# A Macaron block of routed experts and a selective scan: one more pair of buffers for delta*x, whole-group products by B, and a rearranged start

## The chip, the cores and the metric

The kernel runs on one core of a Trainium2 chip, as one launch. The metric is device time in microseconds (us) of one execution; lower is better. The five engines are called by the profile's names: PE (TensorE; PEld is its weight load), DVE (VectorE), ACT (ScalarE), POOL (GpSimd) and SP (SyncE), which here issues DMAs and nothing else.

## What is computed

4096 tokens (2 sequences of 2048) of width 1024 in float32 go through a layer norm and a routed feed-forward, a layer norm and a selective scan, and a third layer norm with the same feed-forward again, each added to its input.

```python
x = x + 0.5 * ffn(layernorm(x), A, B, W, bias)
x = x + scan(layernorm(x), W_xproj, W_dt, b_dt, A_log, D_param)
x = x + 0.5 * ffn(layernorm(x), A, B, W, bias)

def ffn(x, A, B, W, bias):            # A: 64 experts x rank 16 x 1024, top 4 of 64
    vecs = einsum('arh,bsh->bsar', A, x)
    routes = one_hot(top_k(norm(vecs, axis=-1), 4)).sum(-2) / 4
    v = einsum('bsa,bsar->bsr', routes, vecs)
    return x @ W.T + bias + einsum('bsa,ajr,bsr->bsj', routes, B, v)

def scan(x, W_xproj, W_dt, b_dt, A_log, D):   # state 16, rank 128
    xz = x @ W_xproj.T                        # delta_r | B_mat | C_mat
    delta = softplus(delta_r @ W_dt.T + b_dt)
    h_t = exp(delta_t * -exp(A_log)) * h_(t-1) + delta_t * B_t * x_t
    return (sum over n of h_t * C_t) + x * D
```

## The kernel before

**Units.** The work of the two feed-forwards is cut into 64 units of 128 tokens, numbered 0 to 63: 32 of kind 1 (the first feed-forward, and then the projections of the scan) and 32 of kind 2 (the second, on what the scan gives). In a unit a, PE multiplies for the base (`base`, x by W), for the routed part (`routed`, u by B) and, for the next unit b, for the experts (`experts`, x by A). Each weight is held as two float16 parts, high and low, and each product is three: high by high, high by low, low by high. All engines have a hand-written order: `unit(l, a, b)` of each engine's block, with l the unit before.

**Scan groups.** The scan's rows are (channel, state) pairs: a tile t is 128 channels of 512 tokens (64 tiles), and has 4 groups, so there are 256 groups G = 4t + g. A group is four blocks of 128 rows x 512 tokens. Its way: `times_b` (POOL) multiplies delta*x by B into a ring `Hr` of four groups; `decay` (ACT) makes exp(delta*A) into PSUM, two blocks ahead at most; `scan` (DVE) runs the recurrence; `keep_last` (ACT) copies the last column of the four blocks to `hst` for the next chunk and lets `times_c` (POOL) multiply by C in place; `states` (PE) sums over the states into `py`; `sum_up` (DVE) adds x*D. The table that `plan` makes spreads the groups over the units 5 to 57, five a unit in most, four in nine of them (units 5, 10, 16, 22, 28, 34, 40, 46, 52); those of a unit are its slots 0 to 4. POOL does `times_b(G + 2)` ahead of `times_c(G)`.

**The tile's inputs.** delta of tile t is made one or two units ahead: `z` (PE, by a slice of `wdt`, all of W_dt held), `magnitudes` and `softplus` (ACT), `delta` (DVE, which multiplies by the normed x that `load_tile` fetched), `delta_copy`, and `delta_out` (ACT stores delta and delta*x to a scratch in memory, semaphore `s_std`). SP reads them back spread over the partitions: `spread_delta(t, h)` for delta and `spread_inputs(t, h)` for delta*x, in two halves h of 512 KB, each half a pair of blocks. Both rings hold three pairs, `Dr` and `Ur` (`NPR`). So `spread_inputs(t, 1)` overwrites the first pair of tile t - 1, and waits until POOL has multiplied all but the last half group of that tile. With three pairs, a tile's two are not always neighbours, so POOL multiplies in halves in two thirds of the groups:

```python
if g in (1, 2) and pair[0] < pair[1]:
    u = Ur[:, 2 * pair[0]:2 * pair[0] + 4, :]
    pool.tensor_tensor(Hr[:, G % NH, :, :], u, b.broadcast_to([P, 4, CT]), ALU.mult).then_inc(s_bm, 2)
    return
for h in range(2):
    pool.wait_ge(s_ldu[pair[h]], 16 * ((2 * t + h) // NPR + 1))
```

**SP's order in a unit** (`unit` of the sync block): slot 0, the normed tile for z at position 0, `load_x` for the next unit (which waits until that buffer has been stored), the store of the normed x, the two transposes of u (`turn`), slots 1 and 2, the normed tile for z at position 1, the stores of the projections, slots 3 and 4, `load_y`, the unit's result. `slot` issues for group G = 4m + 2: `store_tile`, then `spread_inputs` (both halves) and `spread_delta(t, 0)` of tile t = m + 1; for 4m + 3 `spread_delta(t, 1)`. `plan` gives z of tile t to slot 4t - 6: position 0 of the unit where that is its slot 0, position 1 where it is slot 1 or 2, and position 0 of the next unit where it is slot 3 or 4. Ten units (10, 15, 20, 25, 30, 34, 39, 44, 49 and 54) thus have two z; in all of them the first belongs to slot 3 of the unit before.

**The start.** DVE finds the largest magnitude of A, W and B (`largest`), POOL spreads each over the partitions by a custom instruction (`partition_all_reduce`), DVE makes powers of two of them (`power`, `combine`), ACT makes the high parts of A, W, B in this order (`weight`), and DVE the low parts (`low`), with POOL for the last five of A and the last four of B. PE takes unit 0's experts as the high parts come (`first_experts`), then `first_base` and `first_routed`.

## Time and profile before

| | us |
|---|---|
| median of 3 runs | 2844.78 (2843.44 to 2848.23) |
| the profiled execution | 2852.74 |
| its span, first to last instruction | 2851.0 |
| PE busy | 2604.9 (91%) |
| POOL busy | 2347.1 (82%) |
| DVE busy | 2189.6 (77%) |
| ACT busy | 1448.4 (51%) |

The profiled execution is one run, 7.96 us above the median. The span has three stretches: the start up to about 88 us, in which the weights are prepared and unit 0 is done; units 1 to 4, without scan groups; from 251 us, when POOL starts its first scan group, to 2660 us, when it ends its last, the stretch of the scan, in which all engines are in use; and from there to the end the last units, again without scan groups. A row of a timeline has its start, its length, engine, line, operation, tiles and count, and in brackets how long the engine was idle before it, and what ended that.

### The profile page before, as it was taken

Reading aid. Unit: us, or ns where it says so; the run is one execution under the profiler, and the core shown is the slowest. Engines: PE = TensorE matmul, PEld = TensorE weight load, DVE = VectorE, ACT = ScalarE, POOL = GpSimd, SP = SyncE. Lnnn points to the kernel's source line nnn. Section 1 sums busy time; section 2 is a strip of 40 time slices with the busy share of each in tenths; the row PEclk is TensorE's granted clock in tenths of the full one; section 3 lists DMA queues with packets and bytes.
Section 4 is the critical chain, followed back from the end, with each engine's and each line's share of the span. In section 5 each row is a group of like instructions: output and inputs, shape, how many; then the busy total and the mean of one; then the engine's idle time right before and its main releaser. Section 6 shows DMA issues by size and latency. Waiting matters only on the chain.

```text
span 2851.0 us, 38123 instructions
## 1 busy us (share of the span) xinstructions
PE 2604.9 (91%) x13056; PEld 1158.5 (41%) x13120; DVE 2189.6 (77%) x2661; ACT 1448.4 (51%) x3075; POOL 2347.1 (82%) x703
## 2 busy tenths in 40 slices
PE   4998999999899999989999999999899989988999
PEld 1454444444333434334444343444334433433444
DVE  7434788788888878888888788888888888878533
ACT  5334565555555555545655465555555545454211
POOL 2103999899999999999899999999999999999300
PEclk8999999999999999999999999999999999999999
DMA  5125445554445444554454346444454455444221
GB/s 214 51 62 132 140 133 137 155 154 141 127 131 159 129 129 139 154 137 134 130 167 133 116 131 169 144 127 141 148 148 144 118 157 148 123 137 122 67 60 52
DMA packets 309368, 373.40 MB, mean 131 GB/s; under 512 B 148147, under 2 KB 224051, under 8 KB 309174
## 3 DMA queue, kind: packets, MB, share of 16 engines
q1 hardware_dynamic: 292278, 337.40, 40.7%
q10 hardware_dynamic: 16896, 33.56, 4.0%
q8 instruction: 104, 1.70, 0.2%
q14 instruction: 90, 0.74, 0.1%
HBM read 234.05 MB, written 103.29 MB: 118 GB/s over the span
## 4 chain that ended last, share of the span: by engine, by line
PE 22%; DVE 18%; POOL 10%; DMA 8%; issue 7%; DVEq 5%; ACT 4%; ACTq 1%; SPq 1%; POOLq 0%
DVE mreg L1062 9%; PE pv L491 7%; POOL mreg L459 5%; PE po L491 5%; PE pv L495 3%; POOL mreg L451 3%; DMA delta_scratch<-mreg 3%; PE po L495 3%; DMA mreg<-xnT_scratch 2%; PE py L651 2%; ACT pA L855 1%; POOL mreg L446 1%; DMA uT<-sel 1%; DVE pv L1029 1%; DVE sel L1026 1%
## 5 line engine op out<-in xcount | busy, mean ns | idle before, releaser
L459 POOL TENSOR_TENSOR mreg<-mreg 128x2048 f32<-128x2048 f32 x256 | 1161.1, 4536 | 20.9 <-ACT hst L844 20.7
L1062 DVE TENSOR_TENSOR_SCAN mreg<-pA,hst,mreg 128x512 f32<-128x512 f32 x768 | 940.1, 1267 | 75.5 <-ACT hst L844 45.5
L451 POOL TENSOR_TENSOR mreg<-mreg 128x1024 f32<-128x1024 f32 x340 | 795.8, 2365 | 234.9 <-DMA mreg<-delta_scratch 231.9
L855 ACT ACTIVATE pA<-mreg,nA 128x512 f32<-128x512 f32 x1024 | 696.7, 684 | 467.2 <-DVE mreg L1062 412.9
L491 PE MATMUL po<-wB,uT 128*128 128x512 f16 x2016 | 476.7, 386 | 30.3 <-DMA uT<-sel 16.9
L491 PE MATMUL pv<-wA,xT 128*128 128x512 f16 x2016 | 462.4, 383 | 39.6 <-ACT xT L769 30.5
L491 PE MATMUL po<-wW,xT 128*128 128x512 f16 x2016 | 467.0, 380 | 8.0 <-issue 7.0
L446 POOL TENSOR_TENSOR mreg<-mreg 128x2048 f32<-128x2048 f32 x86 | 390.7, 4544 | 1.6 <-issue 1.6
L1062 DVE TENSOR_TENSOR_SCAN mreg<-pA,cst,mreg 128x512 f32<-128x512 f32 x256 | 313.4, 1267 | 30.4 <-ACT hst L844 20.7
L491 PEld LDWEIGHTS pv<-wA,xT 128*128 128x128 f16 x2016 | 194.0, 99 | 320.6 <-ACT xT L769 76.6
L491 PEld LDWEIGHTS po<-wB,uT 128*128 128x128 f16 x2016 | 192.7, 99 | 321.9 <-issue 94.2
L651 PE MATMUL py<-mreg,Em 128*32 128x512 f32 x2048 | 272.9, 605 | 50.2 <-POOL mreg L459 40.7
L491 PEld LDWEIGHTS po<-wW,xT 128*128 128x128 f16 x2016 | 197.6, 98 | 225.6 <-issue 13.7
L1010 DVE TENSOR_REDUCE n<-sel 128x32 f32<-128x512 f32 x128 | 86.6, 677 | 250.0 <-ACT sel L777 249.9
L495 PE MATMUL pv<-wA,xT 128*128 128x512 f16 x1008 | 243.2, 385 | 27.0 <-DVE xT L1006 27.0
L495 PE MATMUL po<-wB,uT 128*128 128x512 f16 x1008 | 243.2, 385 | 0.0
L495 PE MATMUL po<-wW,xT 128*128 128x512 f16 x1008 | 240.1, 381 | 0.0
L495 PEld LDWEIGHTS pv<-wA,xT 128*128 128x128 f16 x1008 | 98.6, 99 | 150.9 <-issue 36.4
L1042 DVE SCALAR_TENSOR_TENSOR xin<-po,sc,xin 128x512 f32<-128x512 f32 x128 | 92.2, 721 | 85.8 <-PE po L495 82.4
L495 PEld LDWEIGHTS po<-wW,xT 128*128 128x128 f16 x1008 | 94.5, 98 | 151.6 <-issue 45.7
L777 ACT ACTIVATE sel<-pv 128x512 f32<-128x512 f32 x128 | 75.4, 590 | 152.5 <-PE pv L495 148.0
L495 PEld LDWEIGHTS po<-wB,uT 128*128 128x128 f16 x1008 | 100.2, 99 | 108.6 <-issue 6.0
(132 smaller groups left out, 2346.9 us busy)
## 6 DMA issues: line engine op xcount, KB each, us to landing
mreg<-delta_scratch SPq DMA_DIRECT2D x256, 512.0 KB, 5.6
delta_scratch<-mreg ACTq DMA_DIRECT2D x128, 256.0 KB
xin<-x SPq DMA_DIRECT2D x32, 512.0 KB, 4.5
x_scratch<-xin SPq DMA_DIRECT2D x32, 512.0 KB, 7.2
xnT_scratch<-auxs SPq DMA_DIRECT2D x32, 512.0 KB, 2.9
mreg<-xnT_scratch SPq DMA_DIRECT2D x64, 256.0 KB, 6.4
mreg<-bc_scratch SPq DMA_DIRECT2D x64, 256.0 KB, 5.5
yT_scratch<-mreg SPq DMA_DIRECT2D x64, 256.0 KB, 2.4
```

Of the source, the lines that this page charges most:

```text
L446: pool.tensor_tensor(Hr[:, G % NH, :, :], u, b.broadcast_to([P, 4, CT]), ALU.mult).then_inc(s_bm, 2)
L451: pool.tensor_tensor(Hr[:, G % NH, 2 * h:2 * h + 2, :], u, b.broadcast_to([P, 2, CT]), ALU.mult).then_inc(s_bm, 1)
L459: pool.tensor_tensor(h, h, Cr[:, g, :].unsqueeze(1).broadcast_to([P, 4, CT]), ALU.mult).then_inc(s_cm, 1)
L491: last = nc.tensor.matmul(dst, lhs[:, 0, k, :], w[:, wb, k, nb * HF:(nb + 1) * HF], start=(first and k == 0 and wb == 0), stop=False)
L495: last = nc.tensor.matmul(dst, lhs[:, 1, k, :], w[:, 0, k, nb * HF:(nb + 1) * HF], start=False, stop=(stop and k == KD - 1))
L651: last = nc.tensor.matmul(py[32 * s:32 * s + 32, :], Em[:, :], Hr[:, G % NH, s, :], start=(g == 0), stop=(g == 3), tile_position=(0, 32 * s))
L777: nc.scalar.activation(sel[:, nb * HF:(nb + 1) * HF], pv[:, nb, :], ACT.Square).then_inc(s_sq, 1)
L855: nc.scalar.activation(pA[:, i % 2, :], Dr[:, 2 * (n % NPR) + i % 2, :], ACT.Exp, scale=nA[:, c:c + 1]).then_inc(s_dA, 1)
L1010: V.tensor_reduce(n2[:, nb * NE // 2:(nb + 1) * NE // 2], sel3[:, nb * NE // 2:(nb + 1) * NE // 2, :], AX.X, ALU.add)
L1026: V.tensor_tensor(ranked, pv[:, :, :].rearrange("p b (a r) -> p r (b a)", r=R16), mask[:, :].unsqueeze(1).broadcast_to([P, R16, NE]), ALU. ...
L1042: V.scalar_tensor_tensor(dst, po[:, nb, :], sc[:, 3:4], dst, ALU.mult, ALU.add).then_inc(s_res, 1)
L1062: V.tensor_tensor_scan(h, pA[:, i % 2, :], h, before, ALU.mult, ALU.add).then_inc(s_sc, 1)
```

## The change

1. **Four pairs.** `Ur` has four pairs (`NPU`), two tiles' worth, each tile's two side by side. `times_b` is one product of a whole group, waiting for both halves (`s_ldu`, now one semaphore a tile's slot). `spread_inputs` waits for tile t - 2 alone, and both halves are issued in slot 4m + 1 instead of 4m + 2.
2. **`wdt`** holds one tile's slice, 128 x 128. SP loads the next, 64 KB, with `load_dt(t + 1)` in the slot of group 4m = 4(t - 1), and waits there until z of tile t has read the slice in place. z waits for the load (`s_ldw`).
3. **Maxima.** PE spreads the maxima by a product of the column, broadcast, with the identity into `py` (`spread_largest`): A's ahead of `first_experts`, W's and B's together behind it; DVE takes the largest of each row and makes the powers of both at once (`powers`).
4. **Order of the start.** PE takes both parts of x with each slice of A as it comes. ACT does the squares of unit 0 ahead of the weights, then the high parts of W 0 to 4, the choice (`chosen`), W 5 to 7, and B. DVE makes the low parts of W 0 to 4 (two ahead of `gather`) and all of B; POOL those of W 5 to 7 in place of B 4 to 7. PE takes the low part of W after B's high part. The signs and exponents of `nA` and `Em` move behind this.
5. **`decay`** makes the decay of block 1 of a group before, not after, `keep_last` of the group before it.
6. `mask` lies in `n2m`, and the float16 identity is gone.

```diff
-            pool.wait_ge(s_ldu[pair[h]], 16 * ((2 * t + h) // NPR + 1))
-            ...
+                n = t % (NPU // 2)
+                pool.wait_ge(s_e, max(G - NH + 1, 0))
+                pool.wait_ge(s_ldb[g], 16 * (G // NG + 1))
+                pool.wait_ge(s_ldu[n], 32 * (t // (NPU // 2) + 1))
+                b = Br[:, g, :].unsqueeze(1).broadcast_to([P, 4, CT])
+                pool.tensor_tensor(Hr[:, G % NH, :, :], Ur[:, 4 * n:4 * n + 4, :], b, ALU.mult).then_inc(s_bm, 2)
...
+            def load_dt(t):
+                sp.wait_ge(s_z, t)
+                sp.dma_start(wdt[:, :], WdtT[:, t % KD * P:(t % KD + 1) * P]).then_inc(s_ldw, 16)
...
             def spread_inputs(t, h):
-                n = 2 * t + h
+                n = (2 * t + h) % NPU
                 sp.wait_ge(s_std, 32 * (t + 1))
-                sp.wait_ge(s_bm, (8 * (t - 1) if h == 0 else 8 * t - 1) if n >= NPR else 0)
+                sp.wait_ge(s_bm, max(8 * (t - NPU // 2 + 1), 0))
...
+                if G % 4 == 0 and t + 1 < NCH * KD:
+                    load_dt(t + 1)
+                if G % 4 == 1 and t < NGRP // 4:
+                    spread_inputs(t, 0)
+                    spread_inputs(t, 1)
                 if G % 4 == 2:
                     if t >= 2:
                         store_tile(t - 2)
                     if t < NGRP // 4:
-                        spread_inputs(t, 0)
-                        spread_inputs(t, 1)
                         spread_delta(t, 0)
...
+            def spread_largest(lo, hi):
+                pe.wait_ge(s_amx, hi)
+                for n in range(lo, hi):
+                    last = nc.tensor.matmul(py[:, n * P:(n + 1) * P], amm[:, n:n + 1].broadcast_to([P, P]), idf[:, :],
+                                            start=True, stop=True)
+                last.then_inc(s_amr, 1)
...
             def decay(i):
-                if i % 4 == 1 and i > 4:
-                    keep_last(i // 4 - 1)
+                kept = i // 4 - 1 if i % 4 == 1 and i > 4 else None
...
                 nc.scalar.activation(pA[:, i % 2, :], Dr[:, 2 * (n % NPR) + i % 2, :], ACT.Exp, scale=nA[:, c:c + 1]).then_inc(s_dA, 1)
+                if kept is not None:
+                    keep_last(kept)
...
+            def powers(lo, hi, turn):
+                dve.wait_ge(s_amr, turn)
+                V.tensor_reduce(amr[:, lo:hi], py[:, lo * P:hi * P].rearrange("p (n q) -> p n q", q=P), AX.X, ALU.max)
```

SP's queue at the beginning of unit 25, a unit with two z, of the kernel before: the result of unit 24, C's spread, the normed tile for the unit's first z, x of unit 26, the transposes, and further on the two halves of delta*x of tile 25 (L309) and the first of delta (L302).

```order
L408 DMA out<-xin 128x1024 [waits s_res]
L321 DMA mreg<-bc_scratch 128x1x512 [waits s_cm,s_stp]
L332 DMA mreg<-xnT_scratch 128x4x128 [waits s_sty1,s_stn]
L290 DMA xin<-x_scratch 128x1024 [waits s_xn2,s_stx0]
L346 DMA_TRANSPOSE uT<-sel 128x8x128 [waits s_yT,s_u]
L346 DMA_TRANSPOSE uT<-sel 128x8x128 [waits s_u]
L321 DMA mreg<-bc_scratch 128x1x512 [waits s_cm,s_stp]
L337 DMA yT_scratch<-mreg 128x4x128 [waits s_y]
L309 DMA mreg<-delta_scratch 128x1x1024 [waits s_bm,s_std] x2
L302 DMA mreg<-delta_scratch 128x1x1024 [waits s_dA,s_std]
```

The same place with the change (L254 is `load_dt`, L314 `spread_inputs`, L307 `spread_delta`):

```order
L416 DMA out<-xin 128x1024 [waits s_res]
L254 DMA wdt<-WdtT 128x128 [waits s_z]
L326 DMA mreg<-bc_scratch 128x1x512 [waits s_cm,s_stp]
L337 DMA mreg<-xnT_scratch 128x4x128 [waits s_sty1,s_stn]
L295 DMA xin<-x_scratch 128x1024 [waits s_xn2,s_stx0]
L351 DMA_TRANSPOSE uT<-sel 128x8x128 [waits s_yT,s_u]
L351 DMA_TRANSPOSE uT<-sel 128x8x128 [waits s_u]
L314 DMA mreg<-delta_scratch 128x1x1024 [waits s_bm,s_std] x2
```

The load of W_dt's slice, with its wait on PE, now stands ahead of the loads of the normed tile and of x, and the halves of delta*x ahead of the tile's store. The second place is SP's queue at the end of unit 12, where slot 4 is group 37 and the next unit's slot 0 is group 38, before:

```order
L393 DMA bc_scratch<-auxs 32x128
L284 DMA uT<-yT_scratch 128x1024 [waits s_sty1,s_sty2,s_sty0,s_out]
L408 DMA x_scratch<-xin 128x1024 [waits s_res]
L337 DMA yT_scratch<-mreg 128x4x128 [waits s_y]
L309 DMA mreg<-delta_scratch 128x1x1024 [waits s_bm,s_std] x2
```

and with the change:

```order
L401 DMA bc_scratch<-auxs 32x128
L254 DMA wdt<-WdtT 128x128 [waits s_z]
L314 DMA mreg<-delta_scratch 128x1x1024 [waits s_bm,s_std] x2
L289 DMA uT<-yT_scratch 128x1024 [waits s_sty1,s_sty2,s_sty0,s_out]
L416 DMA x_scratch<-xin 128x1024 [waits s_res]
L342 DMA yT_scratch<-mreg 128x4x128 [waits s_y]
```

The halves of delta*x moved past the load of y and the store of the unit's result.

## Rows read from the trace of the kernel before

**Rows 1.** The page's part 1: busy us, share of the span, instructions by engine

```profile
PE 2604.9 (91%) x13056; PEld 1158.5 (41%) x13120; DVE 2189.6 (77%) x2661; ACT 1448.4 (51%) x3075; POOL 2347.1 (82%) x703
```

**Rows 2.** Busy us by engine in the scan's stretch; then granted clock, DMA share, GB/s

```profile
252.00:2660.00 2408.00, 2214.09 (x11210) 971.10 (x11264) 1996.97 (x2364) 1323.03 (x2802) 2322.15 (x682) 0.98 0.48 138
```

**Rows 3.** Groups of instructions (page, part 5): busy, mean ns, idle before and releaser

```profile
L451 POOL TENSOR_TENSOR mreg<-mreg 128x1024 f32<-128x1024 f32 x340 | 795.8, 2365 | 234.9 <-DMA mreg<-delta_scratch 231.9
...
L446 POOL TENSOR_TENSOR mreg<-mreg 128x2048 f32<-128x2048 f32 x86 | 390.7, 4544 | 1.6 <-issue 1.6
```

**Rows 4.** Waits: who for whom, us in total, times, longest

```profile
POOL mreg L451 <- DMA mreg<-delta_scratch: 231.9, 24, 171.5
...
DVE mreg L1052 <- DMA mreg<-xnT_scratch: 48.2, 11, 6.0
...
PE py L651 <- POOL mreg L459: 40.7, 38, 2.8
...
DVE xin L992 <- DMA xin<-x_scratch: 24.9, 7, 5.6
...
DVE mreg L1062 <- POOL mreg L451: 13.9, 11, 2.0
```

**Rows 5.** POOL's timeline: the second half of group 0, and tile 25's first group

```profile
254.80 2.35 POOL L451 TENSOR_TENSOR mreg<-mreg 128x1024 f32<-128x1024 f32 x1 [1.09 <-DMA mreg<-delta_scratch]
...
1194.84 4.66 POOL L451 TENSOR_TENSOR mreg<-mreg 128x1024 f32<-128x1024 f32 x2 [4.93 <-DMA mreg<-delta_scratch]
```

**Rows 6.** The chain that ended last, 1180 to 1460 us: start, length, what

```profile
1179.47 9.73 DMA delta_scratch<-mreg
1189.22 0.53 SPq L309
...
1191.13 6.84 DMA mreg<-xnT_scratch
```

**Rows 7.** The same chain over the whole span by line (page, part 4)

```profile
DVE mreg L1062 9%; PE pv L491 7%; POOL mreg L459 5%; PE po L491 5%; PE pv L495 3%; POOL mreg L451 3%; DMA delta_scratch<-mreg 3%; PE po L495 3%; DMA mreg<-xnT_scratch 2%; PE py L651 2%; ACT pA L855 1%; POOL mreg L446 1%; DMA uT<-sel 1%; DVE pv L1029 1%; DVE sel L1026 1%
```

**Rows 8.** Timeline of PE and DVE: first z of units 10 and 25, y added in 25

```profile
486.15 1.02 PE L638 MATMUL pv<-mreg,wdt 128*128 128x512 f32 x2
...
1166.64 1.02 PE L638 MATMUL pv<-mreg,wdt 128*128 128x512 f32 x2
...
1172.61 0.67 DVE L992 TENSOR_TENSOR xin<-pt,xin 128x512 f32<-128x512 f32 x1
```

**Rows 9.** Timeline of SP's queue: units 10 and 25, end of 26

```profile
487.60 0.37 SPq L326 DMA_DIRECT2D mreg<-delta_rank_scratch  x1
...
1165.20 0.32 SPq L290 DMA_DIRECT2D xin<-x_scratch  x1
...
1248.31 0.34 SPq L408 DMA_DIRECT2D out<-xin  x1
...
1257.38 3.90 SPq L309 DMA_DIRECT2D mreg<-delta_scratch  x2
```

**Rows 10.** DMA issues (page, part 6): KB each, median us from issue to landing

```profile
xin<-x SPq DMA_DIRECT2D x32, 512.0 KB, 4.5
x_scratch<-xin SPq DMA_DIRECT2D x32, 512.0 KB, 7.2
```

**Rows 11.** Timelines of POOL, DVE and ACT in the start, and unit 1's first statistics

```profile
46.70 0.72 POOL L431 PARTITION_ALL_REDUCE amr<-amm  x2 [5.83 <-issue]
...
47.11 0.15 DVE L967 TENSOR_SCALAR sc<-amr 128x1 int32<-128x1 int32 x1 [4.56 <-POOL amr L431]
...
50.56 8.43 ACT L732 ACTIVATE wW<-mreg,sc 128x1024 f16<-128x1024 f32 x8 [17.26 <-DVE sc L1131]
...
80.84 1.27 DVE L983 BATCH_NORM_STATS2 ln_st<-xin 128x6 f32<-128x512 f32 x2
```

**Rows 12.** Groups of instructions: the low parts of B and of W on DVE

```profile
L978 DVE SCALAR_TENSOR_TENSOR wB<-mreg,sc,wB 128x1024 f16<-128x1024 f32 x4 | 11.2, 2862 | 0.0
...
L978 DVE SCALAR_TENSOR_TENSOR wW<-mreg,sc,wW 128x1024 f16<-128x1024 f32 x8 | 9.7, 1278 | 0.6 <-ACT wW L732 0.6
```

More of the change, by code:

```diff
@@ L12 @@
 NPR = 3
+NPU = 4
 NXT = 3
@@ L464, in _ @@
                 low(wA, k, stA[:, k, :]).then_inc(s_loAp, 1)
-            largest(2)
-            largest(1)
-            for k in range(KB, KD):
-                pool.wait_ge(s_scB, k + 1 - KB)
-                low(wB, k, stB[:, k, :] if k < NB5 else stB2[:, k - NB5, :]).then_inc(s_loBp, 1)
+            for k in range(NLW, KD):
+                pool.wait_ge(s_scW, k + 1 - NLW)
+                low(wW, k, stW[:, k, :]).then_inc(s_loWp, 1)
             times_b(0)
@@ L537, in first_base @@
             def first_base(a):
-                pe.wait_ge(s_bsc, 1)
-                for nb in range(2):
-                    nc.tensor.matmul(po[:, nb, :], onesb[:, :], brow[:, nb * HF:(nb + 1) * HF], start=True, stop=False)
                 for k in range(KD):
@@ L546, in first_base, with first_base_low @@
                             nc.tensor.matmul(po[:, nb, :], xT[:, part, k, :], wW[:, 0, k, nb * HF:(nb + 1) * HF],
-                                             start=False, stop=False)
+                                             start=(k == 0 and part == 0), stop=False)
+                pe.wait_ge(s_bsc, 1)
+                for nb in range(2):
+                    nc.tensor.matmul(po[:, nb, :], onesb[:, :], brow[:, nb * HF:(nb + 1) * HF], start=False, stop=False)
+            def first_base_low():
                 for k in range(KD):
-                    pe.wait_ge(s_loW, k + 1)
+                    if k < NLW:
+                        pe.wait_ge(s_loW, k + 1)
+                    else:
+                        pe.wait_ge(s_loWp, k + 1 - NLW)
                     for nb in range(2):
@@ L637, in z @@
                 pe.wait_ge(s_dc, t)
-                nc.tensor.matmul(pz, wdt[:, k * P:(k + 1) * P], drT, start=True, stop=True).then_inc(s_z, 1)
+                pe.wait_ge(s_ldw, 16 * (t + 1))
+                nc.tensor.matmul(pz, wdt[:, :], drT, start=True, stop=True).then_inc(s_z, 1)
             def states(a, n):
@@ L724, in _, with weights_w @@
             act.preload_act_table_set("natural_log_exp_and_others")
+            def weights_w(lo, hi):
+                for k in range(lo, hi):
+                    weight(wW, k, stW[:, k, :], 2, s_hiW, s_scW if k >= NLW else None)
             def weights_b(lo, hi):
                 for k in range(lo, hi):
[L728 removed]
+                    weight(wB, k, stB[:, k, :] if k < NB5 else stB2[:, k - NB5, :], 1, s_hiB)
             def weight(w, k, src, col, s_hi, s_scaled=None):
@@ L928, in _ @@
                 weight(wA, k, stA[:, k, :], 0, s_hiA, s_scA if k >= KD - NB5 else None)
-            act.wait_ge(s_scl, 2)
-            for k in range(KD):
-                weight(wW, k, stW[:, k, :], 2, s_hiW)
-            act.wait_ge(s_cst, 16 * 5)
-            nc.scalar.activation(nA[:, :], nA[:, :], ACT.Exp).then_inc(s_nA, 1)
             squares(US[0], 0)
             squares(US[0], 1)
-            weights_b(0, 2)
+            act.wait_ge(s_scl, 2)
+            weights_w(0, NLW)
             for l, a in zip([None] + US, US):
@@ L978, in low, with lows_w @@
                 return V.scalar_tensor_tensor(w[:, 1, k, :], src, sc[:, col:col + 1], w[:, 0, k, :], ALU.mult, ALU.subtract)
+            def lows_w(lo, hi):
+                for k in range(lo, hi):
+                    low(wW, k, stW[:, k, :], 2, s_hiW).then_inc(s_loW, 1)
             def stats(ln, src, s_done):
@@ L1087, in unit @@
                 if a.u == 0:
-                    for k in range(KB):
-                        low(wB, k, stB[:, k, :], 1, s_hiB).then_inc(s_loB, 1)
+                    lows_w(2, NLW)
+                    for k in range(KD):
+                        low(wB, k, stB[:, k, :] if k < NB5 else stB2[:, k - NB5, :], 1, s_hiB).then_inc(s_loB, 1)
                 scans(2, 5)
@@ L1165, in _ @@
             largest_of(1)
-            power(2)
-            power(1)
+            powers(1, 3, 2)
             combine()
@@ L1170, in _ @@
             V.tensor_scalar(brow[0:3, :], brow[0:3, :], sc[0:3, 12:13], None, ALU.mult).then_inc(s_bsc, 1)
-            for k in range(KD):
-                low(wW, k, stW[:, k, :], 2, s_hiW).then_inc(s_loW, 1)
-            dve.wait_ge(s_id, 2)
-            V.tensor_reduce(Em[:, :], idf[:, :].rearrange("p (j n) -> p j n", n=NN), AX.X, ALU.add)
-            dve.wait_ge(s_nA, 1)
-            V.tensor_scalar(nA[:, :], nA[:, :], -1.0, None, ALU.mult)
-            dve.drain().then_inc(s_set, 1)
             sums(US[0], 0)
```

115 lines of the change are left out of this document (53 added, 62 removed).

## The prediction

> **What bounds the kernel.** I read first the busy times. PE is busy in 91% of the span and POOL in 82% [rows 1], but POOL works in the scan's stretch alone, and there it is busy for 2322.2 of 2408 us, 96.4%, and PE for 2214.1, 92% [rows 2]. So POOL looks like the bound, and 86 us of idleness and its halved products like what can be had back. Then the waits. POOL's wait for delta*x is 231.9 us in 24 times [rows 4]; 171.5 of it is the time until the first group, so 60.4 us in 23 waits lie in the stretch. Then what ends them, tile by tile, from the timelines of POOL and SP. Ten belong to the tiles 7, 13, 19, 25, 31, 36, 42, 48, 54 and 60, the first of the two z of units 10, 15, ... 54, and make up 40 us. There the halves are issued in the very moment when the store of delta has landed, as for tile 25: store until 1189.2, SP's issue at 1189.22 [rows 6], POOL on at 1194.84 after 4.93 us of idleness [rows 5]. Neither the ring nor SP's place in its order holds them; delta is late. 7.8 us belong to tiles 0 and 1, late in the same way, and 13 us to eight others, for which the halves were issued after `sum_up` or after the ring's wait.
>
> Last the chain that ended last, which says what a faster engine would be worth: DVE's scans have 9%, PE's three products (L491, L495) together 18%, and POOL's halves 3%, its whole products by B 1%, its products by C 5% [rows 7]. POOL is busy nearly always, but it is on the path for 9% of the span. The reader should see in these views that POOL and the chain of the units (experts, choice, routed product, norm, on PE, ACT and DVE) run beside each other with little slack, and that it is the second that holds in every unit with two z.
>
> **The change, part by part.** All sums stand against the profiled execution, 2852.7 us; the median of the runs shown is 7.9 us lower.
>
> *The start: -8 us.* DVE has B's maximum at 42.55, POOL's spreading comes at 46.70, and DVE goes on at 47.11 after waiting 4.56 us [rows 11]. On PE the spreading is one weight load and one product a maximum; four such transposes take 1.1 us in this stretch, so DVE goes on at about 43.8. One `powers` for both maxima in place of two saves another 0.9, less 0.4 for the reduction. ACT's first high part of W, at 50.56 [rows 11], comes at 46.3: -4.2 us. Behind this ACT had 8 + 8 high parts, 4 scaled pieces and 3 small steps in 24.1 us at 1.04 each; now it has 16 and 3 scaled pieces, but the choice follows five of them instead of ten, so `gather` begins at 51.9 instead of 64.3, and u is turned at 60.7 instead of 73.0. PE's high part of B (9.1 us) then follows, paced by ACT to 66.4 or by itself to 69.8, then the low parts (3.6 each): end at 75 to 77 for 85.6. DVE ends B's low parts at 61.4 + 8 x 1.28 = 71.6 and starts unit 1's statistics there instead of 80.84 [rows 11]. That is 8.6 to 10 us. A row speaks against this: DVE's low part takes 2862 ns while POOL makes low parts too, and 1278 ns without [rows 12], and W's on POOL (about 54 to 60) touch DVE's from 57.4 on: one or two of DVE's by 1.6. So 7 to 10, and I take 8. The Trainium skill, "SBUF — State Buffer", "Who interferes with whom", says that a DVE instruction with two inputs in SBUF and a GpSimd instruction that reads it exclude each other for a whole instruction. By that rule DVE would be held for all three of POOL's and the start would give 5; it speaks also against products of 4.5 us in place of 2.4, but the scans have one input in PSUM, and take 1267 ns with POOL always busy.
>
> *Whole products: at most -25, I take -9.* Two halves take 2 x 2365 ns and a whole product 4544 [rows 3]; from start to start POOL spends 4.63 us on the pair and 4.48 on the whole, so the 170 pairs save 25 us of its time. It reaches the end only where POOL is followed: PE waited 40.7 us in 38 waits for a product by C, and DVE 13.9 us for one by B [rows 4], in 11 stretches of a few groups each, 10 to 17 groups behind POOL's last stop. There POOL is ahead by 10 to 17 times 0.1, 1.3 us on the mean: 11 x 1.3 = 14. Against it, in the ten late tiles POOL now starts when both halves have landed, about 1 us later, and half of those stretches come right behind such a tile: +5. Bounds: 0 and the 54.6 us that the two waits make together.
>
> *Freed waits: -6.* Of the 13 us of the eight other tiles half, by the same reckoning; 0 to -13. The 40 us of the late tiles stay, because only an earlier delta would end them.
>
> *W_dt by the slice: +13.* In 11 units (5 and the ten with two z) slot 0 is a group 4m whose awaited z is in the same unit. SP, which had issued the normed tile and x of the next unit before it, now stands until z has read. How fast it goes on is in the trace, because the load of the ranks has the same wait in unit 10: z starts at 486.15 [rows 8], SP issues at 487.60 [rows 9], 1.45 us later. Behind it come the slice (0.5), the normed tile (0.6), then x, at z + 2.4, landing 4.5 us later by the median [rows 10], 5.2 where a tile's load was just ahead: z + 7.3. Unit 25 had it issued at 1165.20 [rows 9], 1.4 ahead of z, and DVE added y at 1172.61, z + 6.0 [rows 8]. The seven units of these whose next is of kind 2 (15, 25, 30, 34, 44, 49, 54) add y at z + 4.3 to z + 6.0, so DVE stands for 1.3 to 3 us in each, 15 together. The normed tile lands at z + 7 to z + 9.5, and DVE wants it at z + 8.6 to z + 10.3: 0 to 1 in the other four. The chain goes through DVE there (the 11 waits of 48.2 us for a normed tile [rows 4] are in these units, for their second z), so I count nearly all: +13, with 0 (slack takes it) and +30 (x lands as late as 7 us after its issue, and the tile too) as bounds. The slices themselves (64 KB) are read 18 us or more after their load, and cost nothing.
>
> *Halves in slot 4m + 1: +4.* In eleven units (as 26) this is slot 4, and delta's store lands after the unit's result could be stored: 1248.31 for the result, 1257.38 for the halves, which followed the landing at 1256.7 [rows 9]. Now the result waits behind the halves, about 9 us, and lands 7.2 [rows 10] to 9 later, at about 1266; only then can x of unit 28 be loaded, which was issued at 1262.7 and landed, behind 1.5 MB of other loads, at 1272.3. Those are out of the way now, so it lands at 1270 to 1273. DVE waited for x in six such units, most of the 24.9 us [rows 4], and I reckon -2 to +3 for each: +4 in all, -12 to +18. In the other places SP's wait for delta comes where it stood before.
>
> *First groups: +2.* POOL's product of group 0 ended at 257.1 in halves, with 1.09 of waiting for the second [rows 5]; a whole one ends at 254.8 + 4.5 = 259.3, and DVE was waiting for it. 0 to +3.
>
> *`keep_last` behind `decay`: 0.* DVE's one long wait for a decay a unit (1.44 us) is for block 12, behind ACT's norm, and the swap is in block 13; POOL's product by C comes 0.6 later where it waits for ACT, nine times, each of them a point at which POOL has slack. -3 to +5.
>
> The sum is -8 - 9 - 6 + 13 + 4 + 2 = -4, so 2848.7 for the profiled execution's like and, with the same -4, **2841 us** against the median.
>
> **The rivals.** *POOL is the bound after all.* Then its whole saving returns: 25 for the products, 20 for the waits off the late tiles, some 20 of those at them, since the units would come earlier too, and the start's 8: -73, 2772. For it: 96.4% busy. Against it: the chain, and that PE waits for POOL for 40.7 us only. 12%.
>
> *Slower: SP's wait for z.* It decides if the late x holds DVE in full in the seven units and the late tile in the eleven: 7 x 3 + 11 x 0.8 = 30 in place of 13, and if nothing of POOL's time reaches the end but its share on the chain, 25 x 0.09 = 2, and no freed wait. Then -8 - 2 + 30 + 4 + 2 = +26, 2871. For it: units 10 and 30, in which SP stood for z already, take longer than their like (48.7 us for 45.8 in another of four groups, 50.6 for 48.3). Against it: part of that is the ranks' load. It decides from 23 us lost at z on, 2 a unit: there 8 + 9 + 6 no longer pay for it, the +6 of the rest, and the bound of a measurement. 25%.
>
> *The ring's part does nothing, for delta is late everywhere.* This is half of my forecast; if it held for the eight tiles too, 2847.
>
> **How the numbers follow.** The forecast has 63%, with its own range 2826 to 2856: faster by over 0.2% (5.7 us, about what a measurement of this kernel can tell from no change) in 30, within it in 23, slower in 10 of the 100. With POOL's rival all faster and the second all slower but 2: faster 0.42, same 0.25, slower 0.33. The range that leaves out 2 in 10 drops POOL's rival for the most part and the upper part of the slower one: 2802 to 2868.
>
> **What would show it.** In the profile after: ACT's first high part of W near 46.3, and unit 1's statistics near 72. 256 whole products by B of 4.54 us and none of halves. POOL's waits for delta*x in the ten late tiles, 4 to 5 us each, still there or longer, and nearly none elsewhere. SP's queue at PE's z in eleven units, and DVE's waits for x (L992 in the old lines) more than 24.9 us, with new ones in units 15, 25, 30, 34, 44, 49 and 54. I am wrong if POOL's idleness in the scan's stretch falls under 40 us, or if that stretch is over 30 us shorter or over 20 us longer than 2408.

## The result and the profile after

The changed kernel takes **2874.39 us** (2870.04 to 2874.96, 4 runs) for 2846.26 of the kernel before in the same comparison: ratio **1.0101**, 95% interval 1.0088 to 1.0113. It is slower by 28 us, where 4 less was forecast, and 6 over the upper end of the range.

The page of the changed kernel, part 1 (compare [rows 1]):

```profile
PE 2618.5 (91%) x13062; PEld 1166.1 (41%) x13126; DVE 2186.0 (76%) x2660; ACT 1451.5 (51%) x3074; POOL 2316.5 (81%) x527
```

Its groups on POOL (compare [rows 3]):

```profile
L448 POOL TENSOR_TENSOR mreg<-mreg 128x2048 f32<-128x2048 f32 x256 | 1161.7, 4538 | 277.6 <-DMA mreg<-delta_scratch 265.3 <-issue 12.1
L455 POOL TENSOR_TENSOR mreg<-mreg 128x2048 f32<-128x2048 f32 x256 | 1161.4, 4537 | 44.8 <-ACT hst L852 44.8
```

Its waits (compare [rows 4]):

```profile
POOL mreg L448 <- DMA mreg<-delta_scratch: 265.3, 14, 186.7
...
DVE mreg L1068 <- DMA mreg<-xnT_scratch: 62.0, 11, 6.9
...
DVE xin L1008 <- DMA xin<-x_scratch: 40.0, 12, 6.6
...
PE py L653 <- POOL mreg L455: 12.9, 17, 1.9
```

And the chain that ended last, by engine and by line (compare [rows 7]):

```profile
PE 32%; DVE 27%; DMA 18%; ACT 7%; DVEq 7%; issue 5%; SPq 2%; ACTq 1%; POOL 1%; POOLq 0%
DVE mreg L1078 13%; PE po L484 9%; PE pv L484 9%; DMA delta_scratch<-mreg 7%; DMA yT_scratch<-mreg 5%; PE pv L488 5%; PE po L488 4%; ACT pA L864 3%; DMA xin<-x_scratch 2%; PE py L653 2%; DVEq L1000 2%; PE pv L619 2%; DMA uT<-sel 2%; DVE xT L1022 2%; DVE pv L1045 1%
```

The row by engine of the kernel before:

```profile
PE 22%; DVE 18%; POOL 10%; DMA 8%; issue 7%; DVEq 5%; ACT 4%; ACTq 1%; SPq 1%; POOLq 0%
```

Its shares add up to 76% only: that chain was followed back from the end to about 710 us of the span and no further, so its shares are a third too low beside those of the changed kernel.

POOL has its saving (30 us less busy), but little waits for it now: PE's wait for a product by C went from 40.7 to 12.9 us, and POOL has 1% of the chain for 10% (13% of the part that was followed). DVE waits longer for data: 62.0 for 48.2 us for a normed tile, 40.0 for 24.9 for x. DMAs have more of the chain, 18% for 8: the store of delta, which ACT issues, has 7% for 3, and the store of y, which SP issues, 5%, where it had no row.

The stretch of unit 25 shows both causes. It is the chain of the changed kernel between 1170 and 1200 us, with start, length and what:

```profile
1171.90 0.87 PE pv L638 x2
1172.79 0.34 SPq L254
...
1173.22 0.52 SPq L326
...
1173.85 0.54 SPq L337
...
1174.48 5.57 DMA xin<-x_scratch
...
1180.07 0.69 DVE xin L1008
...
1186.98 8.12 DMA delta_scratch<-mreg
1195.12 0.54 SPq L314
...
1197.00 7.33 DMA yT_scratch<-mreg
```

Read it downward. z's product ends, and only then may SP load the next slice of W_dt (L254). Behind it SP issues C (L326), the normed tile and x; x is added at 1180.07, 8.3 us after z began, where it was z + 6.0 before [rows 8]. Then delta is stored, and the halves (L314) follow its landing. The store of y (L342), which was issued at 1179.46 before, 10 us ahead of the halves, now comes behind them, and the load of the second normed tile waits for the landing of that store.

A table of the units tells where the time lies. A unit's end is the end of its second L1058 on DVE (L1042 before), and lengths are differences of these ends, summed over unit 5 and the ten with two z, over the units behind one in which 4m + 1 is slot 4 (eleven, as unit 27) or slot 3 (thirteen, as unit 28), and over the other 22 up to unit 57:

| profiled execution | end of unit 0 | 11 with two z | 11 behind slot 4 | 13 behind slot 3 | 22 others |
|---|---|---|---|---|---|
| before | 89.4 | 560.2 | 503.3 | 564.4 | 932.5 |
| after | 82.6 | 580.0 | 518.2 | 556.6 | 934.6 |

Seven us are won at the start, 20 lost in the eleven units with two z, 15 lost behind slot 4, 8 won behind slot 3, 2 lost elsewhere: +22 in the profiled execution, whose span is 2873.2. Slots 3 and 4 differ in this: where 4m + 1 is slot 3, 4m + 2 is slot 4 of the same unit (in eleven of the thirteen), so the halves stood ahead of the unit's result before the change too. Only where 4m + 1 is the unit's last slot did they move past it: slot 4, and slot 3 in units 22 and 46, which have four groups.

### The profile page after: what moved, and what is told of

Same layout as the page of the kernel before. It is cut to its first block, busy times and chain, and to the rows that moved or that the text cites. A ratio compares the mean times of both kernels' runs of the same rounds, so it can differ in the third digit from the quotient of the medians.

```text
span 2873.2 us, 38272 instructions
## 1 busy us (share of the span) xinstructions
PE 2618.5 (91%) x13062; PEld 1166.1 (41%) x13126; DVE 2186.0 (76%) x2660; ACT 1451.5 (51%) x3074; POOL 2316.5 (81%) x527
## 3 DMA queue, kind: packets, MB, share of 16 engines
q1 hardware_dynamic: 301350, 341.08, 40.7%
## 4 chain that ended last, share of the span: by engine, by line
PE 32%; DVE 27%; DMA 18%; ACT 7%; DVEq 7%; issue 5%; SPq 2%; ACTq 1%; POOL 1%; POOLq 0%
DVE mreg L1078 13%; PE po L484 9%; PE pv L484 9%; DMA delta_scratch<-mreg 7%; DMA yT_scratch<-mreg 5%; PE pv L488 5%; PE po L488 4%; ACT pA L864 3%; DMA xin<-x_scratch 2%; PE py L653 2%; DVEq L1000 2%; PE pv L619 2%; DMA uT<-sel 2%; DVE xT L1022 2%; DVE pv L1045 1%
## 5 line engine op out<-in xcount | busy, mean ns | idle before, releaser
L448 POOL TENSOR_TENSOR mreg<-mreg 128x2048 f32<-128x2048 f32 x256 | 1161.7, 4538 | 277.6 <-DMA mreg<-delta_scratch 265.3
L455 POOL TENSOR_TENSOR mreg<-mreg 128x2048 f32<-128x2048 f32 x256 | 1161.4, 4537 | 44.8 <-ACT hst L852 44.8
L484 PE MATMUL pv<-wA,xT 128*128 128x512 f16 x2016 | 459.4, 381 | 35.8 <-ACT xT L777 28.4
L1078 DVE TENSOR_TENSOR_SCAN mreg<-pA,cst,mreg 128x512 f32<-128x512 f32 x256 | 313.1, 1266 | 35.5 <-ACT pA L864 33.0
L488 PE MATMUL pv<-wA,xT 128*128 128x512 f16 x1008 | 254.2, 398 | 44.0 <-DVE xT L1022 44.0
L653 PE MATMUL py<-mreg,Em 128*32 128x512 f32 x2048 | 272.7, 604 | 20.4 <-POOL mreg L455 12.9
L1058 DVE SCALAR_TENSOR_TENSOR xin<-po,sc,xin 128x512 f32<-128x512 f32 x128 | 91.9, 718 | 85.9 <-PE po L488 84.4
L999 DVE BATCH_NORM_STATS2 ln_st<-xin 128x6 f32<-128x512 f32 x192 | 122.8, 681 | 8.9 <-DMA xin<-x 3.1
```

The costliest lines, as they stand in the source:

```text
L448: pool.tensor_tensor(Hr[:, G % NH, :, :], Ur[:, 4 * n:4 * n + 4, :], b, ALU.mult).then_inc(s_bm, 2)
L455: pool.tensor_tensor(h, h, Cr[:, g, :].unsqueeze(1).broadcast_to([P, 4, CT]), ALU.mult).then_inc(s_cm, 1)
L484: last = nc.tensor.matmul(dst, lhs[:, 0, k, :], w[:, wb, k, nb * HF:(nb + 1) * HF], start=(first and k == 0 and wb == 0), stop=False)
L488: last = nc.tensor.matmul(dst, lhs[:, 1, k, :], w[:, 0, k, nb * HF:(nb + 1) * HF], start=False, stop=(stop and k == KD - 1))
L653: last = nc.tensor.matmul(py[32 * s:32 * s + 32, :], Em[:, :], Hr[:, G % NH, s, :], start=(g == 0), stop=(g == 3), tile_position=(0, 32 * s))
L999: V.bn_stats(t["st"][:, 6 * n:6 * n + 6], src[:, n * HF:(n + 1) * HF])
```

## The experiments

Ratios are to the kernel before, measured beside each; a difference of two ratios is given in us of 2846, with the two intervals added as squares. Every kernel that starts from the one changed keeps all of it but the lines shown. Where a second slice was wanted, small tensors were packed together to make room.

**First question: SP's wait for z, or the place of the halves?**

```diff
-                sp.wait_ge(s_z, t)
-                sp.dma_start(wdt[:, :], ...
+                sp.wait_ge(s_z, max(t - 1, 0))
+                sp.dma_start(wdt[:, t % 2, :], ...
```

> The changed kernel with two slices of W_dt in place of one, so that SP's load of the next slice waits for the z before the last and never stands; nothing else moves (some small tiles share memory). Theory Z (SP's wait for z is the cost): the normed tile and x of the next unit are issued as early as before, and the time falls by 20 to 28 us, to 2846 to 2854. Theory S (moving the halves of delta*x to slot 4m + 1, ahead of the tile's store of y and of a unit's result, is the cost): it falls by 5 to 12 only, to 2862 to 2869, and DVE's waits for the normed tile of the second z, 62.0 us in 11 times, stay over 50.

Measured: 2860.61, ratio 1.0054 (1.0035 to 1.0073); -13 ± 6 us against the changed kernel. DVE's waits for x fell from 40.0 to 29.3 us; those for the normed tile stayed, at 62.1.

```diff
-                if G % 4 == 1 and t < NGRP // 4:
-                    spread_inputs(t, 0)
-                    spread_inputs(t, 1)
                 if G % 4 == 2:
                     if t >= 2:
                         store_tile(t - 2)
                     if t < NGRP // 4:
+                        spread_inputs(t, 0)
+                        spread_inputs(t, 1)
```

> The changed kernel with both halves of delta*x issued in slot 4m + 2 behind the tile's store, as before the change, with the ring of four, the whole products and the single slice of W_dt kept. Theory Z: hardly better, 2868 to 2875. Theory S: the store of y is out before SP stands for delta, so the second normed tile need not wait for it, and the unit's result goes out as before: 2845 to 2858, DVE's waits for a normed tile back to about 48 us and for x (40.0 us) to under 30.

Measured: 2863.22, ratio 1.0064 (1.0044 to 1.0084); -11 ± 7. The waits for the normed tile fell to 45.9 us, those for x to 23.9. Then both edits, called the repaired kernel from here on:

> Both together: two slices and the halves in slot 4m + 2. Left of the change are the start, the whole products, no wait of the ring, and the swap at the decay. Both theories: under both kernels, 2824 to 2838, that is 2846 less 7 for the start and 4 to 15 for POOL. If it is over 2846, the whole products or the swap cost something that neither theory has.

Measured: 2844.08, ratio 0.9993 (0.9983 to 1.0004); -31 ± 5. Neither theory holds alone, both causes hold, and together they are the loss. Each is worth more with the other gone: two slices 20 ± 6 instead of 13, the old slot 17 ± 6 instead of 11. But the run is 6 us over the range expected for it: what is left of the change is worth -2 ± 3 us, where 8 to 22 were expected.

The profiled executions say where. Lengths are those of the table above; the waits are DVE's for x and for the normed tile, and PE's for the rows of y (`uT`), all in us:

| | two z | behind slot 4 | behind slot 3 | x, in units with two z | x, behind slot 4 | normed tile | rows of y |
|---|---|---|---|---|---|---|---|
| before | 560.2 | 503.3 | 564.4 | 0.0 | 21.4 | 48.2 | 0.0 |
| changed kernel | 580.0 | 518.2 | 556.6 | 7.8 | 29.6 | 62.0 | 10.3 |
| two slices | 565.2 | 512.6 | 556.5 | 0.2 | 27.6 | 62.1 | 8.7 |
| old slot | 575.4 | 492.8 | 565.9 | 14.7 | 9.2 | 45.9 | 0.0 |
| both | 559.6 | 487.2 | 570.1 | 0.0 | 5.5 | 49.2 | 0.0 |

The single slice holds x back in the units with two z (15, 25, 30, 34, 44 and 49 in the run with the old slot), and two slices give these units 15 to 16 us. The early halves hold back x and the rows of y behind slot 4, where the old slot gives 25 us, and the second normed tile; behind slot 3 the old slot takes 9 to 14 us again.

**Second: does the start reach the end, and does the swap cost?** The kernel before with the changed start and with `keep_last` behind `decay`:

> The kernel before with the changed start (maxima by PE, new order of the high and low parts) and the swap of keep_last and decay, but with the ring of three, the halves, the whole W_dt and SP's order of before. If the 7 us by which unit 1 begins earlier reach the end: 2837 to 2841. If the stretch of the scan takes them back, or the swap costs: 2845 or more.

Measured: 2845.59, ratio 1.0004 (0.9992 to 1.0015). Unit 0 ends 6.8 us earlier, and nothing of it was left at the end. So the swap was undone, here and in the repaired kernel:

```diff
-                kept = i // 4 - 1 if i % 4 == 1 and i > 4 else None
+                if i % 4 == 1 and i > 4:
+                    keep_last(i // 4 - 1)
...
-                if kept is not None:
-                    keep_last(kept)
```

> The kernel before with the changed start alone: keep_last stands ahead of decay again (the run before this one, with both, came to 2845.59 for 2846.85 of before, though unit 1 began some 7 us earlier). Theory T, the swap takes the start's gain back: POOL's products by C come 0.6 us later wherever they wait for ACT, and 2837 to 2841 is what the start alone gives. Theory U, the start's gain is taken back in the scan's stretch by itself, since transfers and units meet in another way: then this kernel is within 3 of the run with the swap, 2843 to 2848.

Measured: 2842.89, ratio 0.9987 (0.9978 to 0.9996).

> The changed kernel with two slices of W_dt and the halves of delta*x in slot 4m + 2 (2844.08 with the swap), and keep_last ahead of decay again. Theory T: 2836 to 2840, and POOL's waits for ACT's column copies (19.1 us there) shrink by half. Theory U: 2841 to 2847. The prediction had the swap at 0, with -3 and +5 as bounds.

Measured: 2839.33, ratio 0.9978 (0.9966 to 0.9989). Each is some 4.5 us below its partner, and the two together give 4.5 ± 3: Theory T. POOL's waits for the column copies fell in both, from 27.5 to 20.8 and from 19.1 to 13.6 us, a quarter or a little more and not half. The start alone is worth 3.7 us, half of what it has at unit 0. Part of the rest may lie in the windows of 84 to 124 us, behind the start, of the kernel before and of the start alone (PE, PEld, DVE, ACT, POOL busy, then the granted clock):

```profile
84.00:124.00 40.00, 38.29 (x196) 19.99 (x195) 14.75 (x25) 13.84 (x36) 0.00 (x0) 1.00 0.19 55
```

```profile
84.00:124.00 40.00, 40.00 (x193) 20.22 (x192) 13.89 (x27) 10.82 (x30) 0.00 (x0) 0.95 0.22 68
```

There TensorE ran partly at the lower of its two levels (a mean of 0.95), and unit 1 took 38.1 us for 35.5. The seventeen profiles with the changed start have 1.00 and 35.5 us in four (the changed kernel's among them), and 0.95 to 0.99 and 36.7 to 38.4 us in thirteen. Of the kernel before there is one profile, so it isn't shown that the earlier start brings the lower clock.

**Third: what is a whole product worth?** The repaired kernel, `times_b` in two halves for every group:

> The same repaired kernel (two slices, halves of delta*x in slot 4m + 2; 2844.08) with every product by B made as two halves of a pair each, behind one wait for both. It doubles the number of these instructions and adds some 0.15 us to POOL's time for each of 256 groups, 38 us in all. Theory W, whole products reach the end where PE and DVE follow POOL (in the repaired kernel they wait 89.6 and 44.8 us for it, far more than before): a third of the 38 comes back as time, 2853 to 2860. Theory X, POOL's time is worth nearly nothing because the units' own chain holds: 2843 to 2848. The prediction had the whole products at -9 for 170 of them, which is 2856 or so here.

Measured: 2864.59, ratio 1.0065 (1.0049 to 1.0081), +20 ± 5: Theory W, and more than it asked, half of POOL's 38 us. For the 170 pairs that the change joined it is -13 or so, an estimate by their count.

**Fourth: the loads of the normed tile.** The repaired kernel, in the ten units with two z:

```diff
                         store_tile(t - 2)
+                    if n == 2 and 1 in a.zs:
+                        load_tile(a.zs[1])
```

> The same repaired kernel (2844.08), and in slot 4m + 2 of the ten units with two z SP issues the load of the second normed tile right behind the store of y, ahead of the halves of delta*x, which stand there until delta's store has landed. Theory Y, these loads are on the path of the units with two z (DVE waits 49.2 us in 11 waits for them in the repaired kernel, 62.0 in the changed one, 48.2 in the one before): the waits fall under 15 us, the ten units end 2 to 3 us earlier each, 2818 to 2832. Rival, the wait is cover for another: the time stays at 2840 to 2846 while the waits fall, and DVE or PE wait for POOL or delta instead.

Measured: 2839.6, ratio 0.9974 (0.9963 to 0.9985). (The load is no longer issued at its old place.) The wait is gone from the list, but only 5 ± 4 us came back, as the rival said: DVE waited for POOL's product instead (72.8 us for 44.8). With `keep_last` ahead as well, which is the kernel with both mends:

> The repaired kernel with the second normed tile's load first (2839.6) and keep_last ahead of decay again (2839.33), both. If the two add up against 2844.08: 2834 to 2836. If the one takes the other's room: 2837 to 2841.

Measured: 2843.88, ratio 0.9986 (0.9976 to 0.9995). It is over both ranges: they don't add up, and this is no better than either. Something else held those units.

**Fifth: the rest of the account.**

> The kernel before with the changed start (2842.89 with the swap undone), and W_dt by two slices with their 64 more loads, ring and order as before. The single prices found so far (start -4, swap +4.5, second slice 14, slot 11, whole products -13) leave some 13 of the changed kernel's 28 us open. Theory P, the loads of the slices themselves cost, by SP's issues ahead of the normed tile and x: 2848 to 2856. Theory Q, they are free once they wait for nothing: 2840 to 2845, and what is open lies in the ring of four with its one wait for both halves.

Measured: 2843.84, ratio 0.9985 (0.9975 to 0.9995), as without the slices: Theory Q. 64 more loads cost nothing if SP needn't wait for one.

```diff
-                pool.wait_ge(s_ldu[n], 32 * (t // (NPU // 2) + 1))
+                if g == 0 and t in LATE:
+                    for h in range(2):
+                        pool.wait_ge(s_ldu[2 * n + h], turns)
+                        pool.tensor_tensor(Hr[...2 * h:2 * h + 2...], ...)
+                    return
```

Each half has a semaphore of its own here.

> The kernel with both mends, and in tiles 0, 1 and the ten late ones group 0's product by B is made in two halves again, each behind its own half's landing, as in the kernel before. Theory Q: POOL starts some 1 us earlier in each of the late tiles and is followed there by PE and DVE, so it ends 5 to 12 us before the run with both mends. Theory P: within 2 of it, since 0.15 more for the split stands against the earlier start and delta's store is what the tile waits for.

Measured: 2826.76, ratio 0.9921 (0.9904 to 0.9939), 18 ± 6 us below its partner, more than Theory Q expected. Tile 25 shows why: SP's issue of the two halves and POOL's first product, from the timelines (start, length, what, idle before and releaser). With one wait for both:

```profile
1181.23 1.17 SPq L316 DMA_DIRECT2D mreg<-delta_scratch  x2
```

```profile
1188.04 4.51 POOL L451 TENSOR_TENSOR mreg<-mreg 128x2048 f32<-128x2048 f32 x1 [4.83 <-DMA mreg<-delta_scratch]
```

```profile
1192.58 2.46 DVE L1078 TENSOR_TENSOR_SCAN mreg<-pA,hst,mreg 128x512 f32<-128x512 f32 x2 [3.86 <-POOL mreg L451]
```

and in halves:

```profile
1175.38 1.17 SPq L316 DMA_DIRECT2D mreg<-delta_scratch  x2
```

```profile
1180.74 4.66 POOL L456 TENSOR_TENSOR mreg<-mreg 128x1024 f32<-128x1024 f32 x2 [2.21 <-DMA mreg<-delta_scratch]
```

```profile
1185.43 2.46 DVE L1090 TENSOR_TENSOR_SCAN mreg<-pA,hst,mreg 128x512 f32<-128x512 f32 x2 [2.56 <-POOL mreg L456]
```

DVE's scan waits for the whole group in both, and starts 11.4 us from the issue with one wait and 10.1 in halves. Over the ten late tiles, from the issue to POOL's start and to the group's end, each worked out as in these rows: 4.7 and 9.7 us before, 7.0 and 11.5 in the changed kernel, 7.2 and 11.7 with both mends, 5.1 and 10.0 with the half start. The halves land 1.2 to 4.3 us apart, about 2 on the mean, and the first one's product fills the time until the second is there.

> The changed kernel, but for tiles 1, 7, 13, ... 60 (the first of two z in their unit) the halves of delta*x are issued in slot 4m + 2 behind the store of y, as before; the other 52 tiles keep slot 4m + 1. Theory V, the slot costs through the store of y in the units with two z, since the second normed tile's load waits for it: nearly the whole 11 comes back, 2861 to 2866, and DVE's waits for the normed tile fall from 62.0 to 48 or so. Theory R, the slot costs through the unit's result, which stands behind the halves in the eighteen units where 4m + 1 is slot 3 or 4: 2870 to 2876, and DVE's waits for x stay near 40.

Measured: 2874.61, ratio 1.0092 (1.0075 to 1.0109): -3 ± 6, Theory R (there are 24 such tiles, not eighteen). DVE's waits for the normed tile did fall, from 62.0 to 50.1 us, and the eleven units only from 580.0 to 577.1. Then the other way round, with only those 24 tiles put back:

> The changed kernel, but for the tiles for which slot 4m + 1 is slot 3 or 4 of its unit the halves of delta*x are issued in slot 4m + 2 as before; all others keep slot 4m + 1. Theory R, the slot costs through the unit's result, which stands behind halves that wait for delta's store, and so through the next x: 2862 to 2867, and DVE's waits for x fall from 40.0 to 25 or so. Rival, it costs everywhere a little (the store of y, the order of the loads among each other): 2868 to 2874.

Measured: 2855.87, ratio 1.0045 (1.0016 to 1.0074): -16 ± 9, below both ranges. The slot's whole cost lies where it is slot 3 or 4, and the units say that it is slot 4: the eleven behind slot 4 take 492.4 us for 518.2, the thirteen behind slot 3 560.9 for 556.6. SP's queue in the changed kernel at the end of unit 26, whose slot 4 it is:

```profile
1244.99 0.34 SPq L254 DMA_DIRECT2D wdt<-WdtT  x1
1264.33 1.17 SPq L314 DMA_DIRECT2D mreg<-delta_scratch  x2
1265.67 0.47 SPq L289 DMA_DIRECT2D uT<-yT_scratch  x1
1266.19 0.53 SPq L416 DMA_DIRECT2D out<-xin  x1
1266.76 0.53 SPq L342 DMA_DIRECT2D yT_scratch<-mreg  x1
```

and with these tiles put back:

```profile
1240.91 0.32 SPq L291 DMA_DIRECT2D uT<-yT_scratch  x1
1248.86 0.34 SPq L421 DMA_DIRECT2D out<-xin  x1
1256.13 0.37 SPq L344 DMA_DIRECT2D yT_scratch<-mreg  x1
1258.28 1.18 SPq L316 DMA_DIRECT2D mreg<-delta_scratch  x2
...
1260.83 0.55 SPq L297 DMA_DIRECT2D xin<-x_scratch  x1
```

For 19 us SP stands at the halves. The two traces are 8.4 us apart by then (unit 26 ends at 1257.23 and at 1248.83), so the issues are read against the unit's end. The rows of y are issued 8.4 us after it instead of 7.9 before it, 16.4 later; the unit's result 9.0 after it instead of at once, 8.9 later; the store of y 9.5 for 7.3, 2.2 later. The changed kernel's chain goes on from there:

```profile
1266.76 10.01 DMA yT_scratch<-mreg
1276.83 0.37 SPq L337
1277.29 5.11 DMA xin<-x_scratch
1282.43 0.69 DVE xin L1008
```

The next normed tile has the place of the one that is being stored (the ring has three), so SP holds its load (L337) until the store of y has landed, which took 10.0 us here, between other transfers, and 2.9 with the tiles put back. x stands behind that load: it is issued 20.1 us after the unit's end for 12.0, and lands 25.2 after it for 22.0. DVE waits 6.6 us for it in unit 27 for 3.5, and the unit takes 49.7 for 46.6. Over the eleven units behind slot 4 DVE's waits for x fell from 29.6 to 13.3 us and PE's for the rows of y from 10.3 to nothing, which together is about the 25.8 us that these units gave. The line of the latter in the changed kernel:

```profile
PE pt L476 <- DMA uT<-yT_scratch: 10.3, 6, 2.9
```

The eleven with two z took 586.7, 6.7 longer. DVE's waits for x there are 3.6 us of it; the rest isn't explained.

> The changed kernel, and in tiles 0, 1 and the ten late ones group 0's product by B in two halves, each behind its own half's landing, as before. If the one wait for both halves is what is left of the loss (14 + 11 + 4.5 for slice, slot and swap, 13 given back by whole products, 4 by the start, 28 measured, so some 15 open): 2857 to 2863. If it costs only where POOL is followed, as in the repaired kernel (PE waited 99.4 us for POOL there and 12.9 in the changed one): 2868 to 2874, and the prices depend on each other.

Measured: 2869.62, ratio 1.0083 (1.007 to 1.0096): -5 ± 5. That is the second of the two: the one wait costs less in the changed kernel, though not clearly less than the 9 ± 5 of the next run. (The 99.4 us are those of the kernel with both mends; the repaired kernel has 89.6.)

> The repaired kernel with keep_last ahead of decay (2839.33) and the half start in tiles 0, 1 and the ten late ones, without the second tile's load ahead of the halves. If the half start gives its 17 us by itself: 2821 to 2826. If it needs the load first, because DVE otherwise waits for the normed tile (47.4 us in 11 waits there): 2830 to 2837.

Measured: 2830.55, ratio 0.9946 (0.9932 to 0.996), 9 ± 5 below its partner. So the half start gives 9 alone and 18 behind the tile's earlier load: by these values each was cover for the other, though the two intervals touch.

> The kernel with both mends and the half start (2826.76), and group 0 of all 64 tiles in two halves, each behind its own landing. It adds 52 splits of 0.15, 8 us of POOL's time, half of which reached the end in the run with halves everywhere: 2829 to 2833. If an earlier first pair helps DVE in every tile: 2820 to 2825.

Measured: **2822.43**, ratio **0.9918** (0.9905 to 0.9932), the lowest time here. Against its partner (0.9921) it can't be told apart; the expected rise of 2 to 6 didn't come. Its units with two z take 533.7 us, for 560.2 before.

## Why the prediction was wrong

*The start: -8, and 3.7 ± 2.6 by the runs.* The steps were right: DVE goes on at 43.92 (about 43.8 was said), ACT's first part of W is at 47.00 (46.3) and unit 1's statistics at 73.66 (72), for 80.84 [rows 11]. POOL's low parts and DVE's meet: DVE's at 57.90 and 59.83, beside the last of POOL's (58.78), take 2.01 and 3.14 us in place of 1.28, and that one of POOL's 3.11 for 2.13. By the Trainium skill, "SBUF — State Buffer", "Who interferes with whom", a DVE instruction with two inputs in SBUF and a GpSimd instruction that reads SBUF contend for a shared port, which is locked and not divided. The trace agrees with such a lock: DVE lost 2.6 us beside the one and a half that overlapped, and not what all three would have cost. What failed is that the 7 us at unit 0 were carried to the end undiminished.

*Whole products: -9, made of -14 for the saving and +5 for the one wait.* The -14 was near: it is -13 by the run with halves everywhere. But that run starts from the repaired kernel; in the changed one, where PE waits 12.9 us for POOL and not 89.6, the saving wasn't measured. The +5 is the 5 ± 5 of the changed kernel by luck: the step had POOL start "when both halves have landed, about 1 us later", and it is 7.0 for 4.7 us behind the issue, 2.3 later, with the group ready at 11.5 for 9.7. That is 1.8 us in each of ten tiles, 18 together. The other delays of the changed kernel seem to hide most of it; in the repaired kernel the wait is worth 9 ± 5, and 18 ± 6 when the second normed tile is early too. The price of group 0 was near: POOL starts it at 248.63 and ends at 253.1 for 257.1, while all units came 6.9 earlier, so 2.9 later for the 2.2 reckoned.

*Freed waits: -6.* Nothing of it was seen at the end. POOL's waits for delta*x in the scan's stretch are 265.3 - 186.7 = 78.6 us in 13 times, for 60.4 in 23: ten stops went, and the late ones got longer.

*W_dt by the slice: +13, and 13 ± 6 by the runs, 20 ± 6 with the halves in their old slot.* Mechanism and place were right. With the halves in their old slot DVE waits 14.7 us for x in six of the seven units named, and not at all with two slices; the step said 15. The normed tile behind the slice never held DVE, as said: DVE's eleven waits for a normed tile are all for the second one, and their growth to 62.0 us belongs to the halves, since it stays with two slices (62.1) and goes with the old slot (45.9).

*Halves in slot 4m + 1: +4, and 11 ± 7 by the runs, 17 ± 6 with two slices.* This is the step whose mechanism failed. Its place was right: the loss is in the units behind the eleven in which 4m + 1 is slot 4 (25.8 us against the run with the tiles put back), and the others, of which it said that "SP's wait for delta comes where it stood before", lose nothing. Its delay of the result was right too, about 9 us. But it had x go out as soon as the result had landed, and land no later than before (24.0 us after unit 26's end). It left out two transfers that the halves now hold back, the rows of y and the store of y. In SP's order the next normed tile's load stands ahead of x and waits for the landing of that store. So x lands 25.2 us after the unit's end, and PE waits 10.3 us in all for the rows of y, for which it never waited. With the tiles put back x lands at 22.0: the four pairs spare SP its stop between the two halves (3.90 us for both in [rows 9], 1.18 in that run), and the early halves took this gain away again.

*`keep_last` behind `decay`: 0, and 4.5 ± 3.* The upper bound, +5, was the better value: POOL's waits for ACT's copies, which grow with the swap by 6.7 and 5.5 us, were taken to fall where POOL has slack.

*The sum.* The miss is 32 us, and it has two parts. The two steps that cost, slice and halves, were put at 17 and are worth 31 ± 5 together. All the rest was put at -21 (start -8, whole products -9, freed waits -6, first groups +2, `keep_last` 0) and is worth -2 ± 3, the repaired kernel against the one before. Its single prices fit that: start -4, `keep_last` +4.5, whole products -13, the one wait +9, which is -3.5. So over half of the miss are savings that didn't come: half of the start's, all of the freed waits', and what the one wait took back from the whole products.

By its own sign the prediction was wrong as well: POOL's stretch, from 248.63 to 2682.24, is 2433.6 us long, over 20 longer than 2408. The slower rival (25%, 2871) was nearest in time, but by luck: it gave 30 us to SP's wait for z, which is worth 13 or 20, and 4 to the early halves, which are worth 11 or 17. POOL as the bound fell in this kernel. But the 9% of the chain, which was followed for 76% of the span only, and PE's 40.7 us of waiting were no measure of what POOL could be worth: in the repaired kernel PE waits 89.6 us for it, and half of what was added to POOL's time reached the end.

## What to carry to other kernels

A queue that issues in order makes each of its waits a wait of everything behind it. When an issue is moved forward, list everything that it now stands ahead of, also what is only stored, and follow each to the next load that waits for it and to what stands behind that load. Give a load that must follow a read a second buffer: the same 64 loads cost nothing with two slices (-1 ± 4 us) and 13 to 20 us with one. And a larger instruction that waits for more operands gives back what it saves where the operands are late: whole products gave 13 us, and the first group of the late tiles, in halves behind their own landings, another 9 to 18 in the repaired kernel and 5 ± 5 in the changed one. Last, sum up what a change saves as sceptically as what it costs: a start that was 7 us shorter gave 4 at the end.

## What the runs showed that was not expected

Behind the shorter start TensorE's granted clock was below 1.00 in thirteen of seventeen profiles (0.95 to 0.99 on the mean of 84 to 124 us), and unit 1 took 1.2 to 3.0 us longer. The one profile of the kernel before has 1.00 there. This may be where part of the start's saving went; it isn't shown.

Two waits in the same units hid each other. With `keep_last` ahead of `decay`, the second tile's earlier load alone gave nothing (+2 ± 4 us) and the half start alone 9 ± 5; together they gave 16 ± 6.
